# Soft mixture of layer 3: the gate by ScalarE's silu straight into the kept rows, in place of tanh and a product on VectorE

## The chip, the cores and the metric

One core of a Trainium2 chip runs the whole kernel. The metric is the device time of one execution in microseconds. The engines are TensorE (PE in the profile), VectorE (DVE), ScalarE (ACT), GpSimd (POOL) and SyncE (SP), which issues the transfers.

## The reference

Four layers, each `x = x + s * g`, with `s` a mixer over the normalized `x` and `g = silu(f)` with `f` a feed-forward part. `x` is 8 sequences of 512 tokens with 128 features, in float32. In layer 3, `s` is an attention with 16 heads and `f` a soft mixture of 16 experts with 16 slots each:

```python
def _L3_ffn_ref(x, ln_gamma, ln_beta, mu, scale, w1, b1, w2, b2):
    xn = _layernorm(x, ln_gamma, ln_beta)
    x_unit, mu_unit = _l2norm(xn, axis=-1), _l2norm(mu, axis=0)
    logits = jnp.einsum('bnd,des->bnes', x_unit * scale, mu_unit)
    dispatch = jax.nn.softmax(logits, axis=1)
    combine = jax.nn.softmax(logits.reshape(B, N, E * S), axis=-1).reshape(B, N, E, S)
    slot_in = jnp.einsum('bnd,bnes->besd', xn, dispatch)
    h = jax.nn.gelu(jnp.einsum('besd,edh->besh', slot_in, w1) + b1[None, :, None, :], approximate=False)
    slot_out = jnp.einsum('besh,ehd->besd', h, w2) + b2[None, :, None, :]
    return jnp.einsum('besd,bnes->bnd', slot_out, combine)
...
s = _L3_attn_ref(xn, ...)
g = _silu(_L3_ffn_ref(xn, ...))
x = x + s * g
```

## The kernel before

The layers run one after the other. Layer 3 has two stages with a barrier of all engines between them: first the soft mixture (`m3_pe`, `m3_dve`, `m3_act`, `m3_pool`), which leaves the gate of all 8 sequences in `gate3`, then the attention heads (`heads_*`), and at the end `heads_close`, which multiplies the sum over the heads by the gate and adds it to `x`.

The mixture is a pipeline over slots 0 to 13 (`m3_slots`). One sequence `b` goes through it, and in each slot every engine does one step each of several sequences, in an order written out by hand. Waits are semaphore counts: `m3_filled` and `m3_emptied` for the banks of PSUM, and one count for each other kind of result. Buffers are two, taken in turn by `b % 2` (`lanes_m`).

ScalarE's order in slot s is: `open_copy(s-2)` (the transposed rows, L2644), `dispatch_copy(s-2)` (L2674), `combine(s-2)` (four exps with their sums, L2658), `slots_copy(s-2)` (L2680), `units_copy(s-1)` (L2650), `gelu(s-2)` (four, L2686), `dispatch(s-1)` (two exps, L2667), `square(s)` (L2640), `tanh(s-4)` (L2694). A step is left out where its sequence is not one of 0 to 7: so the last `combine` and `gelu` are in slot 9, the last `dispatch` in slot 8, and the gates of sequences 0 to 7 in slots 4 to 11. The program names no tables of ScalarE here; the compiler puts the loads ahead of the functions that need another table.

TensorE's order in a slot is: `slot_logits(s-1)`, `combine_turn(s-2)`, `outputs(s-3)`, `token_logits(s-1)`, `opened_rows(s-1)`, `dispatch_turn(s-1)`, `slots(s-1)`, `slot_out(s-2)`, `units(s)`, `hidden(s-1)`. Of these `slots` waits for ScalarE's `dispatch_copy`, `hidden` for its `slots_copy`, and `slot_logits` for its `units_copy`. Behind the slots stand 16 products of the value and output weights for the heads, in banks 2 to 5, which ScalarE copies out (L2717).

VectorE, in its order, has `dispatch_scale`, `total` (L2542), `token_max`, `moments`, `unit_rows`, `scale`, `gate`, `gamma` (L83), `slot_bias` (L2587), `slot_max` (L2568 and L88), `combine_copy` (L2582) and `divide` (L2596), which writes `f`. GpSimd has `own_expert` (L2782), which stands between gelu and `slot_out`, and small powers.

The gate before is made from tanh: `silu(f) = 0.5 f (1 + tanh(f / 2))`. ScalarE's `tanh(b)` reads `f` (in `sT`) and writes `th` (in `aT`) once `divide(b)` is done and the product of sequence b - 2 has read the buffer. VectorE's `gate(b)` two slots later writes `(th + 1) * f` to `gate3`, twice the gate, and `heads_close` has the factor 0.5.

Of the kernel before, what the change touches and what calls it, by code (L numbers as in the profile page):

```python
# [45 lines left out]
class Kernel:  # L46
# [2186 lines left out]
    def layer3_prepare(self):  # L2233
# [8 lines left out]
        k.own, k.mu_scratch = k.sb("own", [P, 2, P]), k.sb("mu_scratch", [P, 2, 256])  # L2242
        both = k.acc.rearrange("p (two h) t d -> p two (h t) d", two=2)
        k.wv3, k.wo3 = both[:, 0, :, :], both[:, 1, :, :]
        k.m3_mom, k.m3_r, k.m3_norm, k.m3_gt = (n.again() for n in (k.moments, k.rstds, k.scaled, k.gated))
        k.m3_rr, k.m3_xg, k.m3_xb = (Count(nc, n) for n in ("m3_rr", "m3_xg", "m3_xb"))
        k.m3_sq, k.m3_ss, k.m3_ru, k.m3_xu, k.m3_mx, k.m3_ms = (
            Count(nc, n) for n in ("m3_sq", "m3_ss", "m3_ru", "m3_xu", "m3_mx", "m3_ms"))
# [31 lines left out]
        for j in range(2):  # L2280
            half = slice(512 * j, 512 * j + 512)
            quarter = slice(256 * j, 256 * j + 256)
            k.lanes_m.append(dict(
                cmb=flat[:, 1024 * j:1024 * j + 1024].rearrange("p (t c) -> p t c", t=TPB),
                dspT=flat[:, 2048 + 1024 * j:3072 + 1024 * j].rearrange("p (h s) -> p h s", h=2),
                dsp=flat[:, 4096 + 1024 * j:5120 + 1024 * j].rearrange("p (t c) -> p t c", t=TPB),
                cT=flat[:, 6144 + 1024 * j:7168 + 1024 * j].rearrange("p (h s) -> p h s", h=2),
                xn=flat[:, 8192 + 512 * j:8704 + 512 * j].rearrange("p (t d) -> p t d", d=D),
                hT=flat[:, 9216 + 512 * j:9728 + 512 * j],
                g=flat[:, 10240 + 512 * j:10752 + 512 * j].rearrange("p (g s) -> p g s", g=4),  # L2290
                f=k.sT[:, half].rearrange("p (t d) -> p t d", d=D), th=k.aT[:, half].rearrange("p (t d) -> p t d", d=D),
                slotT=k.hT[:, quarter], so=k.hT[:, 512 + 256 * j:768 + 256 * j].rearrange("p (h d) -> p h d", h=2)))
            rows = k.sb(f"m3_rows{j}", [P, 28])
            k.m3_rows.append(dict(r=rows[:, 0:4], r2=rows[:, 4:8], ss=rows[:, 8:12], ru=rows[:, 12:16], mx=rows[:, 16:20],
                                  tot=rows[:, 20:24], ms=rows[:, 24:26], ssum=rows[:, 26:28]))
# [202 lines left out]
    def m3_dve(self):  # L2498
# [97 lines left out]
            V.tensor_tensor(k.lanes_m[j]["f"], k.bank(0).rearrange("p (t d) -> p t d", d=D),  # L2596
                            tot.unsqueeze(2).broadcast_to([P, TPB, D]), ALU.mult).then_inc(*k.m3_emptied[0].up())

        def gate(b):
            t = k.lanes_m[b % 2]  # L2600
            V.wait_ge(k.m3_th.sem, b + 1)
            k.stt(k.gate3[:, b * TPB:(b + 1) * TPB, :], t["th"], 1.0, t["f"], ALU.add, ALU.mult).then_inc(*k.m3_gt.up())

        for s in k.m3_slots():
            if 0 <= s - 3 < SEQS:
                dispatch_scale(s - 3)
            if 0 <= s - 2 < SEQS:
                total(s - 2)
            if 0 <= s - 3 < SEQS:
                token_max(s - 3)  # L2610
            if 0 <= s < SEQS:
                moments(s)
            if 0 <= s - 2 < SEQS:
                unit_rows(s - 2)
            if 0 <= s - 1 < SEQS:
                scale(s - 1)
            if 0 <= s - 6 < SEQS:
                gate(s - 6)
            if 0 <= s - 1 < SEQS:
                gamma(s - 1)  # L2620
            if 0 <= s - 4 < SEQS:
                slot_bias(s - 4)
            if 0 <= s - 2 < SEQS:
                slot_max(s - 2)
            if 0 <= s - 3 < SEQS:
                combine_copy(s - 3)
            if 0 <= s - 4 < SEQS:
                divide(s - 4)

    def m3_act(self):  # L2630
        k, A = self, self.A

        def square(b):
            j = b % 2
            A.wait_ge(k.m3_xb.sem, b + 1)
            k.after(A, k.m3_ss, b - 1)
            if b == 0:
                k.m3_emptied_of(A, 7, "directions")
                A.activation(k.mu_scratch[:, 1, :], k.mu_scratch[:, 1, :], ACT.Sqrt).then_inc(*k.m3_length.up())
            A.activation(k.normed[:, j * TPB:(j + 1) * TPB, :], k.lanes_m[j]["xn"], ACT.Square).then_inc(*k.m3_sq.up())  # L2640

        def open_copy(b):
            k.m3_filled_by(A, 0, "open", b)
            A.activation(k.nT3[:, b, :], k.bank(0), ACT.Identity).then_inc(*k.m3_emptied[0].up())  # L2644

        def units_copy(b):
            k.m3_filled_by(A, 1, "units", b)
            k.m3_filled_by(A, 2, "token_logits", b - 2)
            k.m3_filled_by(A, 4, "slot_logits", b - 2)
            A.activation(k.lanes_m[b % 2]["hT"], k.bank(1), ACT.Identity).then_inc(*k.m3_emptied[1].up())  # L2650

        def combine(b):
            t, r = k.lanes_m[b % 2], k.m3_rows[b % 2]
            A.wait_ge(k.m3_mx.sem, b + 1)
            k.m3_filled_by(A, 2, "combine_turn", b - 2)
            k.m3_emptied_of(A, 0, "outputs", b - 2)
            for i in range(TPB):
                m = A.activation(t["cmb"][:, i, :], k.bank(2 + i // 2)[:, i % 2 * 256:i % 2 * 256 + 256], ACT.Exp,  # L2658
                                 bias=r["mx"][:, i:i + 1], accum_out=r["tot"][:, i:i + 1])
            m.then_inc(*k.m3_emptied[2].up())  # L2660

        def dispatch(b):
            t, r = k.lanes_m[b % 2], k.m3_rows[b % 2]
            A.wait_ge(k.m3_ms.sem, b + 1)
            k.m3_filled_by(A, 4, "dispatch_turn", b - 2)
            for h in range(2):
                m = A.activation(t["dspT"][:, h, :], k.bank(4 + h), ACT.Exp, bias=r["ms"][:, h:h + 1],  # L2667
                                 accum_out=r["ssum"][:, h:h + 1])
            m.then_inc(*k.m3_emptied[4].up())

        def dispatch_copy(b):
            k.m3_filled_by(A, 4, "dispatch_turn", b)
            k.m3_filled_by(A, 1, "slots", b - 2)
            A.activation(k.lanes_m[b % 2]["dsp"].rearrange("p t c -> p (t c)"),  # L2674
                         k.bank(4, 2).rearrange("p a c -> p (a c)"), ACT.Identity).then_inc(*k.m3_emptied[4].up())

        def slots_copy(b):
            k.m3_filled_by(A, 1, "slots", b)
            k.m3_filled_by(A, 6, "hidden", b - 2)
            A.activation(k.lanes_m[b % 2]["slotT"], k.bank(1)[:, 0:256], ACT.Identity).then_inc(*k.m3_emptied[1].up())  # L2680

        def gelu(b):
            k.m3_filled_by(A, 6, "hidden", b)
            k.m3_filled_by(A, 7, "slot_out", b - 2)
            for g in range(4):
                m = A.activation(k.lanes_m[b % 2]["g"][:, g, :], k.bank(6)[:, g * P:(g + 1) * P], ACT.Gelu,  # L2686
                                 bias=k.b1s[:, g:g + 1])
            m.then_inc(*k.m3_emptied[6].up())

        def tanh(b):  # L2690
            t = k.lanes_m[b % 2]
            k.m3_emptied_of(A, 0, "outputs", b)
            k.after(A, k.m3_gt, b - 1)
            A.activation(t["th"], t["f"], ACT.Tanh, scale=0.5).then_inc(*k.m3_th.up())  # L2694

        for s in k.m3_slots():
            if 0 <= s - 2 < SEQS:
                open_copy(s - 2)
            if 0 <= s - 2 < SEQS:
                dispatch_copy(s - 2)  # L2700
            if 0 <= s - 2 < SEQS:
                combine(s - 2)
            if 0 <= s - 2 < SEQS:
                slots_copy(s - 2)
            if 0 <= s - 1 < SEQS:
                units_copy(s - 1)
            if 0 <= s - 2 < SEQS:
                gelu(s - 2)
            if 0 <= s - 1 < SEQS:
                dispatch(s - 1)  # L2710
            if 0 <= s < SEQS:
                square(s)
            if 0 <= s - 4 < SEQS:
                tanh(s - 4)
        for bank in (2, 4):
            k.m3_filled_by(A, bank, "products", bank)
            A.activation(k.wvo[:, 4 * bank - 8:4 * bank, :], k.bank(bank, 2).rearrange("p a (t c) -> p (a t) c", c=D),  # L2717
                         ACT.Identity).then_inc(*k.m3_emptied[bank].up())
# [418 lines left out]
    def heads_close(self):  # L3137
        k, V = self, self.V
        for b in range(SEQS):
            x, s = k.xs[:, b * TPB:(b + 1) * TPB, :], k.acc[:, b, :, :]  # L3140
            V.wait_ge(k.h_acc.sem, k.UNITS - SEQS + b + 1)
            k.step(k.stt(s, s, 0.5, k.gate3[:, b * TPB:(b + 1) * TPB, :], ALU.mult, ALU.mult))
            V.tensor_tensor(x, x, s, ALU.add).then_inc(*k.dve.up())  # L3143
            k.Y.wait_ge(k.dve.sem, k.dve.n)
            k.Y.dma_start(k.io["out"][b].rearrange("(t p) d -> p t d", p=P), x).then_inc(*k.stored.up(16))
# [136 lines left out]
```

## Time and profile before

| | before |
|---|---|
| three executions | 3347.18, 3357.71, 3360.47 us; median 3357.71 |
| the profiled execution | 3347.59 us, span 3345.5 us |
| TensorE, VectorE, ScalarE, GpSimd busy | 93%, 76%, 51%, 25% of the span |
| mixture of layer 3 (1645 to 1775 us of the span) | TensorE 104.9, VectorE 94.0, ScalarE 88.1, GpSimd 54.9 us busy |
| granted clock of TensorE, mean | 0.964 |

The span reaches from the first to the last instruction; the profiled execution took 2.1 us more than its span. Times in the rows are from the start of the span. An engine is busy while it computes, not while it waits for a semaphore.

### The profile page before, as it was taken

What the parts mean: (1) busy time and instruction counts of PE and PEld (TensorE: products, weight loads), DVE (VectorE), ACT (ScalarE), POOL (GpSimd) and SP (SyncE); (2) the same over time, 40 slices, a digit from 0 to 9 for tenths busy, and PEclk for the clock granted to TensorE, in tenths of its full rate; (3) what the DMA queues carried; (4) which work ended last, traced back from release to release, by engine and by line L of the source; (5) the groups of instructions that cost most, each with busy time, mean ns of one, the idle gap of its engine ahead of it and who ended that gap; (6) DMA issues with size and microseconds to landing.
All of it is one profiled execution on the core that took longest, in us unless ns stands there. A gap on an engine that the chain in (4) does not pass through costs nothing. (4 is left out here: it accounts for less than half of the span.)

```text
span 3345.5 us, 57578 instructions
## 1 busy us (share of the span) xinstructions
PE 3112.3 (93%) x20342; PEld 2428.7 (73%) x20342; DVE 2532.5 (76%) x5359; ACT 1702.1 (51%) x3928; POOL 851.6 (25%) x706
## 2 busy tenths in 40 slices
PE   5999998979788789999789999999999999999998
PEld 4777674545454567778577888888888888888887
DVE  4878775858677755555586888888888888888888
ACT  2545543222212144443375666666666666666666
POOL 2101000010101020000243344444444444444443
PEclk9999998989898999998899999999999999999999
DMA  2001101000000000000300010000010110000000
GB/s 53 2 5 51 45 7 48 0 1 1 1 1 0 1 1 1 1 1 1 78 1 1 22 22 22 14 17 15 20 22 22 22 22 9 17 18 22 22 1 26
DMA packets 43552, 53.05 MB, mean 16 GB/s; under 512 B 8645, under 2 KB 27272, under 8 KB 43272
## 3 DMA queue, kind: packets, MB, share of 16 engines
q1 hardware_dynamic: 39298, 47.02, 5.6%
q8 instruction: 167, 2.74, 0.4%
q10 hardware_dynamic: 3974, 2.37, 0.3%
q14 instruction: 113, 0.93, 0.1%
HBM read 38.63 MB, written 10.75 MB: 15 GB/s over the span
## 5 line engine op out<-in xcount | busy, mean ns | idle before, releaser
L75 PE MATMUL banks<-scratch 128*128 128x128 f32 (+3 forms) x3648 | 717.2, 325 | 11.5 <-ACT scratch L2674 8.9
L75 PE MATMUL banks<-nT,w 128*128 128x512 f32 x1184 | 585.5, 613 | 52.7 <-DVE hidden L1562 35.4
L75 PEld LDWEIGHTS banks<-scratch 128*128 128x128 f32 x3648 | 483.9, 192 | 77.4 <-issue 59.7
L75 PEld LDWEIGHTS banks<-scratch,tb 128*128 128x128 f32 x2560 | 356.6, 191 | 101.9 <-issue 61.5
L75 PE MATMUL banks<-scratch,tb 128*128 128x128 f32 x2560 | 368.6, 275 | 0.0
L3117 POOL TENSOR_TENSOR scratch<-scratch,aT 128x1024 f32<-128x1024 f32 x128 | 358.7, 2803 | 4.5 <-DVE aT L2939 4.5
L75 PEld LDWEIGHTS banks<-nT,w 128*128 128x128 f32 x1184 | 204.7, 196 | 212.9 <-issue 145.4
L83 DVE SCALAR_TENSOR_TENSOR scratch<-scratch,tb 128x512 f32<-128x512 f32 (+3 forms) x512 | 339.8, 705 | 8.3
L83 DVE SCALAR_TENSOR_TENSOR scratch<-tb,nn,banks 128x512 f32<-128x512 f32 (+3 forms) x512 | 267.6, 543 | 76.3 <-PE banks L75 72.2
L3109 POOL TENSOR_TENSOR scratch<-backwards,nn 128x512 f32<-128x512 f32 x128 | 133.0, 1039 | 735.7 <-ACT nn L3029 735.7
L2939 DVE TENSOR_TENSOR aT<-banks,turn 64x1024 f32<-64x1024 f32 x256 | 312.9, 1222 | 5.7
L3052 ACT ACTIVATE scratch<-banks 128x384 f32<-128x384 f32 (+1 forms) x384 | 199.7, 520 | 183.5 <-PE banks L79 183.5
L3043 ACT ACTIVATE scratch<-scratch,mn 128x512 f32<-128x512 f32 (+3 forms) x512 | 282.6, 566 | 0.4 <-DVE mn L2973 0.2
L2929 DVE TENSOR_TENSOR scratch<-banks,turn 128x512 f32<-128x512 f32 x256 | 176.1, 688 | 137.7 <-PE banks L75 136.5
L1527 ACT ACTIVATE gated_h<-banks 128x512 f32<-128x512 f32 x160 | 95.5, 597 | 332.2 <-PE banks L75 238.4
L2973 DVE CUSTOM_DVE_ANT_0 scratch<-scratch,tb,coef 128x512 f32<-128x512 f32 (+3 forms) x512 | 261.3, 547 | 0.0
L75 PEld LDWEIGHTS banks<-minus_half,sT 128*128 128x128 f32 x2048 | 239.0, 192 | 2.0 <-ACT sT L3022 2.0
L75 PE MATMUL banks<-minus_half,sT 128*128 128x1 f32 x2048 | 236.1, 245 | 1.2 <-ACT sT L3018 1.2
L79 PEld LDWEIGHTS banks<-ident,scratch 128*128 128x128 f32 x1408 | 171.0, 141 | 73.4 <-issue 69.6
L79 PE MATMUL banks<-ident,scratch 128*128 128x128 f32 x1408 | 219.2, 273 | 3.3 <-DVE scratch L88 2.0
L3035 ACT ACTIVATE scratch<-scratch 128x384 f32<-128x384 f32 (+1 forms) x384 | 215.0, 560 | 8.1 <-DVE scratch L83 6.4
L88 POOL TENSOR_SCALAR rstd<-mv 128x4 f32<-128x4 f32 x40 | 9.9, 247 | 815.6 <-DVE mv L1018 391.1
(393 smaller groups left out, 5367.3 us busy)
## 6 DMA issues: line engine op xcount, KB each, us to landing
tb<-head_rows SPq DMA_DIRECT2D x32, 512.0 KB, 7.1
turn<-head_turns SPq DMA_DIRECT2D x64, 128.0 KB, 2.7
head_turns<-loads SPq DMA_DIRECT2D x16, 256.0 KB, 2.9
head_turns<-rotation SPq DMA_DIRECT2D x16, 256.0 KB, 2.9
xs<-in_x SPq DMA_DIRECT2D x8, 256.0 KB
w<-in_L_Wqk SPq DMA_DIRECT2D x16, 128.0 KB, 2.1
out<-xs SPq DMA_DIRECT2D x8, 256.0 KB, 2.3
w<-in_L_w1T SPq DMA_DIRECT2D x1, 1280.0 KB, 9.2
```

The costliest lines, as they stand in the source:

```text
L75: return self.T.matmul(out, lhsT, rhs, start=start, stop=stop, skip_group_check=True)
L79: return self.T.matmul(out, in_, self.ident[0:n, 0:n], start=start, stop=True, is_transpose=True, skip_group_check=True)
L83: return self.V.scalar_tensor_tensor(out, a, s, b, op0, op1)
L1527: A.activation(k.gated_h[:, u % 2, :], k.bank(2 * (u % 3)), ACT.Tanh, scale=0.5).then_inc(*k.l1_tanh.up())
L2929: V.tensor_tensor(t["qk"][:, i * S:(i + 1) * S], k.bank(2 + i), hd["turn"][:, 0, :], ALU.mult).then_inc(*(k.h_ck if i else k.h_cq).up())
L2939: x = V.tensor_tensor(k.sines[there, :].rearrange("p (i s) -> p i s", i=2), k.bank(2, 2)[here, :, :], hd["turn"][here, 1, :].unsqueeze(1). ...
L2973: x = V.tensor_tensor_reduce(y, y, view(hd["tb"][:, 2, i * P + 127:i * P + 128], [[-1, n]]), k.coef[:, h:h + 1], 3e38, ALU.add, ALU.min, t ...
L3035: A.activation(y, y, ACT.Ln, bias=1.0).then_inc(*k.h_ln.up())
L3043: x = A.activation(y, y, ACT.Exp, bias=t["mn"][:, i:i + 1], scale=-1.0, accum_out=t["sum"][:, i:i + 1])
L3052: A.activation(t["pt"][:, lo:hi], k.bank(7 if piece == 1 else 6)[:, 0:hi - lo], ACT.Identity).then_inc(*k.h_pt.up())
L3109: G.tensor_tensor(t["dk"][:, :, :], k.backwards[:, :].unsqueeze(1).broadcast_to([P, 4, P]), t["nn"][:, 4:8].unsqueeze(2).broadcast_to([P, ...
L3117: G.tensor_tensor(t["qk"], t["qk"], k.sines, ALU.add).then_inc(*k.h_rot.up())
```

## The change

`gate(b)` on VectorE goes. ScalarE's `tanh(b)` becomes `gate(b)`: one silu of `f`, written straight into the rows of `gate3`, which nothing reads before `heads_close`. It waits for `divide(b)` as before and no longer for VectorE's product of sequence b - 2. The buffer `th` and the count `m3_gt` go, and `heads_close` has the factor 1.0. `divide` still waits until ScalarE has read `f` of sequence b - 2.

```diff
-        def gate(b):
-            t = k.lanes_m[b % 2]
-            V.wait_ge(k.m3_th.sem, b + 1)
-            k.stt(k.gate3[:, b * TPB:(b + 1) * TPB, :], t["th"], 1.0, t["f"], ALU.add, ALU.mult).then_inc(*k.m3_gt.up())
...
-            if 0 <= s - 6 < SEQS:
-                gate(s - 6)
...
-        def tanh(b):
+        def gate(b):
             t = k.lanes_m[b % 2]
             k.m3_emptied_of(A, 0, "outputs", b)
-            k.after(A, k.m3_gt, b - 1)
-            A.activation(t["th"], t["f"], ACT.Tanh, scale=0.5).then_inc(*k.m3_th.up())
+            A.activation(k.gate3[:, b * TPB:(b + 1) * TPB, :], t["f"], ACT.Silu).then_inc(*k.m3_th.up())
...
             if 0 <= s - 4 < SEQS:
-                tanh(s - 4)
+                gate(s - 4)
...
-            k.step(k.stt(s, s, 0.5, k.gate3[:, b * TPB:(b + 1) * TPB, :], ALU.mult, ALU.mult))
+            k.step(k.stt(s, s, 1.0, k.gate3[:, b * TPB:(b + 1) * TPB, :], ALU.mult, ALU.mult))
```

## Rows read from the trace of the kernel before

**Rows 1.** The page, busy us and share of the span.

```profile
PE 3112.3 (93%) x20342; PEld 2428.7 (73%) x20342; DVE 2532.5 (76%) x5359; ACT 1702.1 (51%) x3928; POOL 851.6 (25%) x706
```

**Rows 2.** Busy time by stretch: PE, PEld, DVE, ACT, POOL, clock, DMA share, GB/s.

```profile
1645.00:1775.00 130.00, 104.86 (x643) 86.59 (x644) 93.97 (x242) 88.05 (x195) 54.94 (x91) 0.94 0.16 42
```

**Rows 3.** Timeline of ScalarE, one slot: start us, us, line, names, [idle before, releaser].

```profile
1717.74 1.02 ACT L2674 ACTIVATE scratch<-banks 128x1024 f32<-128x1024 f32 x1 [0.28 <-PE banks L79]
1718.66 0.47 ACT L2658 ACTIVATE scratch<-banks,m_rows 128x256 f32<-128x256 f32 x1
...
1720.36 0.22 ACT L2658 ACTIVATION_READ_ACCUMULATOR scratch<-banks,m_rows 128x1 f32 x1
1720.85 0.38 ACT L2680 ACTIVATE hT<-banks 128x256 f32<-128x256 f32 x1 [0.26 <-PE banks L75]
1722.18 0.60 ACT L2650 ACTIVATE scratch<-banks 128x512 f32<-128x512 f32 x1 [0.94 <-PE banks L79]
1722.79 1.28 ACT L2686 ACT_TABLE_LOAD   x1
1724.09 1.14 ACT L2686 ACTIVATE scratch<-banks,b1s 128x128 f32<-128x128 f32 x4
...
1727.88 0.62 ACT L2640 ACTIVATE normed<-scratch 128x512 f32<-128x512 f32 x1
1728.40 0.62 ACT L2694 ACTIVATE aT<-sT 128x512 f32<-128x512 f32 x1
1729.99 0.60 ACT L2644 ACTIVATE nT<-banks 128x512 f32<-128x512 f32 x1 [0.97 <-PE banks L79]
1730.87 1.02 ACT L2674 ACTIVATE scratch<-banks 128x1024 f32<-128x1024 f32 x1 [0.28 <-PE banks L79]
```

**Rows 4.** Timeline of TensorE in that slot: `slots`, `units`, `hidden`, `slot_logits`.

```profile
1718.82 1.99 PE L75 MATMUL banks<-scratch 128*128 128x256 f32 x8 [1.11 <-ACT scratch L2674]
...
1721.54 0.60 PE L79 MATMUL banks<-ident,moe 128*128 128x128 f32 x4
1721.98 1.06 PE L75 MATMUL banks<-hT,w1s 128*128 128x128 f32 x8
1722.87 1.94 PE L75 MATMUL banks<-scratch,mu 128*128 128x512 f32 x4
```

**Rows 5.** Timeline of VectorE in that slot: the product, `slot_max`.

```profile
1721.82 0.68 DVE L83 SCALAR_TENSOR_TENSOR gate<-aT,sT 128x512 f32<-128x512 f32 x1
...
1724.85 1.22 DVE L2568 TENSOR_REDUCE m_rows<-banks 128x2 f32<-128x1024 f32 x1 [0.74 <-PE banks L75]
1726.11 0.17 DVE L88 TENSOR_SCALAR m_rows<-m_rows 128x2 f32<-128x2 f32 x1
```

**Rows 6.** Groups by line, 1645 to 1775 us, and by tile: busy us, mean ns.

```profile
L2667 ACT ACT_TABLE_LOAD x8 | 10.3, 1283 | 0.1
L2686 ACT ACT_TABLE_LOAD x8 | 10.3, 1283 | 0.1
...
L2694 ACT ACTIVATE aT<-sT 128x512 f32<-128x512 f32 x8 | 5.0, 628 | 5.0 <-DVE sT L2596 5.0
...
L83 DVE SCALAR_TENSOR_TENSOR gate<-aT,sT x8: 676/680/691, 1708.7 to 1770.3; 128x512 f32<-128x512 f32 x8
```

**Rows 7.** Timelines of the tail: ScalarE, TensorE (`hidden(7)`, `slot_out(7)`), VectorE.

```profile
1760.62 0.38 ACT L2680 ACTIVATE hT<-banks 128x256 f32<-128x256 f32 x1 [0.26 <-PE banks L75]
...
1762.41 1.14 ACT L2686 ACTIVATE scratch<-banks,b1s 128x128 f32<-128x128 f32 x4
...
1761.31 1.06 PE L75 MATMUL banks<-hT,w1s 128*128 128x128 f32 x8
...
1765.04 1.16 PE L75 MATMUL banks<-w2s,scratch 128*128 128x128 f32 x8
...
1765.73 0.68 DVE L83 SCALAR_TENSOR_TENSOR gate<-aT,sT 128x512 f32<-128x512 f32 x1
1766.33 0.42 DVE L2587 TENSOR_TENSOR hT<-banks,b2s 128x256 f32<-128x256 f32 x1
```

**Rows 8.** The page, DMA issues: KB each, us to landing.

```profile
tb<-head_rows SPq DMA_DIRECT2D x32, 512.0 KB, 7.1
```

More of the change, by code:

```diff
@@ L2244, in layer3_prepare @@
         k.wv3, k.wo3 = both[:, 0, :, :], both[:, 1, :, :]
-        k.m3_mom, k.m3_r, k.m3_norm, k.m3_gt = (n.again() for n in (k.moments, k.rstds, k.scaled, k.gated))
+        k.m3_mom, k.m3_r, k.m3_norm = (n.again() for n in (k.moments, k.rstds, k.scaled))
         k.m3_rr, k.m3_xg, k.m3_xb = (Count(nc, n) for n in ("m3_rr", "m3_xg", "m3_xb"))
@@ L2290, in layer3_prepare @@
                 g=flat[:, 10240 + 512 * j:10752 + 512 * j].rearrange("p (g s) -> p g s", g=4),
-                f=k.sT[:, half].rearrange("p (t d) -> p t d", d=D), th=k.aT[:, half].rearrange("p (t d) -> p t d", d=D),
+                f=k.sT[:, half].rearrange("p (t d) -> p t d", d=D),
                 slotT=k.hT[:, quarter], so=k.hT[:, 512 + 256 * j:768 + 256 * j].rearrange("p (h d) -> p h d", h=2)))
```

## The prediction

> **What bounds the kernel now.** I read the page first. TensorE is busy 93% of the span [rows 1], so a change elsewhere counts only where TensorE waits for it. The table of stretches gives the soft mixture of layer 3 about 130 us out of 3345.5 us, with VectorE at 94.0 and ScalarE at 88.1 us busy in it [rows 2]. Nothing else of the program is touched, apart from a constant (0.5 to 1.0) in `heads_close`, which costs the same. So the question is what sets the length of a slot of this stage.
>
> The timeline of one middle slot answers it. I call its start D: the moment where ScalarE begins `dispatch_copy`, 1717.74, and again 1730.87 in the next slot: a period of 13.13 us [rows 3]. TensorE has one wait in a slot, 1.11 us, for `dispatch_copy` [rows 4]; the rest of the period is its own work end to end, from `slots` over `units`, `hidden`, `slot_logits` to the next `dispatch_turn`. Whatever delays one of these by some time lengthens the slot by that time. ScalarE waits four times in a slot, before `open_copy` 0.97, `dispatch_copy` 0.28, `slots_copy` 0.26 and `units_copy` 0.94 us. One activation starts about 0.10 us ahead of the end of the one before (1717.74 + 1.02 against 1718.66) [rows 3], so the room at each wait is 0.10 us more.
>
> **The work that goes.** Eight `gate` products on VectorE, 0.68 us each [rows 6], at most 5.4 us. In the slot shown the product at 1721.82 stands ahead of `gamma`; behind both VectorE still waits 0.74 us for TensorE's `slot_logits` [rows 5], and TensorE waits for neither. I take nothing for seven of them. If one of VectorE's results set the slot, each would give up to 0.6 us: that is the lower bound. In the tail one counts: the product at 1765.73 holds back `slot_bias(7)` until 1766.33, though `slot_out(7)` is done at 1765.04 + 1.16 = 1766.20 [rows 7]. With 0.04 us for the signal it could start at 1766.24: a gain of 0.09 us. The activation itself stays: eight tanh of 628 ns [rows 6] become eight silu on the same 128x512. I price silu as tanh; an identity of this shape has 0.60 us and the squaring 0.62 us [rows 3], so the function hardly shows in the duration. ScalarE's wait for the product of sequence b - 2 goes too; it never showed as a wait. The stored gate goes straight into rows that nobody reads before the end, so no new wait arises.
>
> **What it adds.** Table loads. Exp and gelu alternate in this stage, and each change has a load of 1283 ns, eight and eight [rows 6]. Tanh has no load of its own at any of its eight places [rows 6], five with exp's table loaded, as in the slot shown [rows 3], and three with gelu's behind the last gelu: both tables have it. Silu does not run in this kernel, so the rows don't show where it lives. Between "as tanh" (no load) and "as gelu" (a load to it and one back), I take the second: a function with a curve of its own, as gelu is.
>
> The order on ScalarE is: combine (exp), gelu, dispatch (exp), squaring, gate. With silu, there is a load ahead of the gate in slots 4 to 9 (in slots 10 and 11 silu is loaded already), and one ahead of combine in slots 5 to 9: 11 loads more. One switch costs the load and the lost overlap: gelu starts 1724.09 - 1722.18 = 1.91 us after `units_copy` rather than 0.50, so 1.41 us [rows 3]. All of it on the path would be 11 x 1.41 = 15.5 us, the upper bound at this price.
>
> The row shows one load of 1.28 us between the copy and gelu, and 0.03 us beside it. The Trainium skill, ScalarE: Activation LUTs, What ACT_TABLE_LOAD costs, has some 2.66 us for a switch, half of it a drain of the engine. The trace agrees with its 1283 ns and shows no such drain. By its price the sum would be +13 us, by the row's the +2.1 us below.
>
> **Step by step in a middle slot, from D.** Combine's first exp moves from D + 0.92 to D + 2.33. The last accumulator read of combine began at 1720.36 = D + 2.62, and the next work can start 0.09 us later, D + 2.71; with the load D + 4.12, where `slots_copy` started at D + 3.11. It ends at D + 4.50, and 0.06 us later (the signal, as 1718.76 to 1718.82) TensorE can start `hidden`: D + 4.56, against 1721.98 = D + 4.24 [rows 3, 4]. So 0.32 us late. `units_copy` could start at D + 4.12 + 0.28 = D + 4.40, before its units are there (D + 4.44): no delay. `slot_logits` goes 0.32 us later with TensorE, then `slot_max` on VectorE, which ended at 1726.11 + 0.17 = D + 8.54 [rows 5]; now D + 8.86, so dispatch starts at D + 8.90 rather than D + 8.80 and pushes the squaring and gate by 0.10 us. The silu load adds 1.41 us: `open_copy` could start at 1728.40 + 0.10 + 1.41 + 0.52 = 1730.43, `dispatch_copy` 0.50 us later, 1730.93 = D + 13.19. TensorE, late by 0.32 us, lets it start only at D + 13.45 [rows 3]. So the silu load is hidden, by 0.26 us, and the load for exp costs 0.32 us a slot.
>
> Slots 5 to 8 have both: 4 x 0.32 = 1.28 us. Slot 4 has the silu load alone: `dispatch_copy` could start at 1730.83 where it started at 1730.87, in the terms of the slot shown: hidden by 0.04 us.
>
> In slot 9 the chain is another [rows 7]: `slots_copy(7)`, gelu(7), `own_expert(7)`, `slot_out(7)`, `slot_bias(7)`, `outputs(7)`, the products of the values. `slots_copy(7)` starts 1.01 us later than 1760.62, ends at 1762.01; the gelu load behind it lets gelu start at 1763.32, against 1762.41 [rows 7]: 0.91 us. Less the 0.09 us at `slot_bias`: 0.82 us. Sum: 1.28 + 0.82 = +2.1 us. VectorE's last products lie beside TensorE's products of the values and end before them, so nothing is gained at the barrier.
>
> The profiled execution has a span of 3345.5 us and took 3347.6 us; it becomes 3349.7 us. That execution stands at the low end of what was run (3347.2 to 3360.5 us), 10.1 us below the median of 3357.7 us. On the median the forecast is 3359.8 us. A measurement of this kernel can't tell under about 0.5% (16.8 us) from no change.
>
> **The rivals.**
>
> *No switch at all.* Silu is in the table that exp uses. Only the 0.09 us at `slot_bias` goes, and perhaps two tenths in slots where VectorE is last: 3357.4 us; with all eight products on the path 5.4 us, 3352.3 us. For it: tanh does just this. Against it: gelu does not, and goes back and forth at every change. Chance 0.12.
>
> *ScalarE becomes the bound.* Its four waits with 0.10 us each leave 2.45 + 0.40 = 2.85 us of room, and two switches take 2.82 us [rows 3]. The period would be 13.13 - 2.85 + 2P for a price P of a switch, beyond the 13.45 us that TensorE sets from P = 1.6 us. If the engine also stood still for as long as a load lasts, P = 2 x 1.283 = 2.57 us, the period would be 15.4 us: 4 x 2.3, with 1.1 us more in slot 4 (2.57 less the 1.45 us of cover there) and 2.0 us in the tail (0.82 and the 1.16 us by which P is dearer) 12.3 us, 3370.0 us. Against it: all 16 loads of the stage last 1283 ns and what follows starts at once. Also here: a load placed ahead of the squaring, which would hold VectorE's `total`; the loads shown stand directly ahead of the function that needs them. Chance 0.08. The Trainium skill's price for a switch (same page and section, an estimate from its 2.66 us) would give 3371 us by the same way.
>
> *Slower by over 0.5%: the load of silu's table is a dear one.* If only the six loads of silu cost Q, the slot is 13.13 - 2.85 + 1.41 + Q = 11.69 + Q, and the whole 4 x (11.69 + Q - 13.13) + (Q - 1.45) + 0.82 = 5Q - 6.4 us. It decides (16.8 us) from Q = 4.6 us. The price could come from a fetch from memory, as a 512 KB transfer with 7.1 us [rows 8]: Q = 1.3 + 7.1 = 8.4 us, +36 us, 3393 us. Against it: the loads of two tables in these rows last 1283 ns alike [rows 6]. The Trainium skill, same page and section, has such a refill by DMA where a program uses more than 8 sets. No run here shows one, and the kernel calls only exp, logarithm, sine, gelu, square root and tanh beside silu. Chance 0.03.
>
> *Faster by over 0.5%.* The stage would need to lose 16.8 us; the removed work is 5.4 us. Only a drift between the measurements does this. Chance 0.02.
>
> **How the numbers follow.** Forecast 0.75, no switch 0.12, ScalarE as bound 0.08, dear load 0.03, faster 0.02. The first three lie within 0.5% and hold 0.95; 0.01 of it goes to slower for drift between measurements: same 0.94, slower 0.04, faster 0.02. The range: the executions of before scatter over 13 us around the same work, so the low end is a low execution with no cost, 3346, and the high end the highest one with half of the bound of 15.5 us, 3360.5 + 7.7 = 3368.
>
> **What would show it.** In the changed profile: six loads at the gate's line and five at combine's, with 8 + 8 as before; a middle slot of 13.45 us (13.13 for no switch, over 15 for a dear switch); the wait of `hidden` for `slots_copy`, about 0.3 us, in three or four slots; `dispatch_copy` still waiting for TensorE; ScalarE's busy time in the stage up by 14 us; VectorE's down by 5.4 us; the heads starting 2.1 us later in the span. I am wrong if the loads stand elsewhere than directly ahead of their function, if silu's activation is longer than 0.63 us by more than 0.26 us, or if there are no new loads.

## The result and the profile after

The changed kernel has a median of 3359.66 us (3354.74 to 3364.81, 22 runs); the kernel before, run between them, 3353.57 us (3347.18 to 3367.18, 22 runs). The ratio is 1.0018, with a 95% interval of 1.0011 to 1.0025: 3.7 to 8.4 us slower, in the band that was called "same", and inside the range. The forecast of 3359.8 us for the median hits by luck: it was 3357.7 us, the median of the three runs known then, plus 2.1 us. The median of before is 3353.6 us over 22 runs, and the change costs more than 2.1 us.

Page of the changed kernel: its span and the first part, to be held against [rows 1].

```profile
span 3358.1 us, 57575 instructions
PE 3123.1 (93%) x20342; PEld 2432.5 (72%) x20342; DVE 2527.6 (75%) x5351; ACT 1717.2 (51%) x3939; POOL 851.1 (25%) x706
```

The profiled span is 12.6 us longer, and most of this is not the change. In the profiled executions TensorE's first matmul of the mixture (`directions`) starts at 1640.6 us before and at 1649.9 us after, behind the same instructions; over all twelve experiments it lies between 1641 and 1655 us, in no order that has to do with the edits. The heads, from their first matmul to the end, take 1571.7 us in both. So I compare the stage alone.

Groups by line of ScalarE, 1645 to 1780 us, changed kernel; the gate is L2686, combine L2651, gelu L2679, dispatch L2660. The last two rows are the gate by tile.

```profile
L2660 ACT ACT_TABLE_LOAD x8 | 10.3, 1283 | 0.1
L2679 ACT ACT_TABLE_LOAD x8 | 10.3, 1283 | 0.1
...
L2686 ACT ACT_TABLE_LOAD x6 | 7.7, 1283 | 0.1
L2651 ACT ACT_TABLE_LOAD x5 | 6.4, 1283 | 0.1
...
L2686 ACT ACTIVATE gate<-sT x8: 629/631/632, 1711.6 to 1782.2; 128x512 f32<-128x512 f32 x8
L83 DVE SCALAR_TENSOR_TENSOR acc<-acc,gate x8: 660/684/685, 3344.1 to 3354.3; 128x512 f32<-128x512 f32 x8
```

Against [rows 6]: six loads at the gate and five at combine, 11 as forecast, each 1283 ns; silu 631 ns, tanh had 628; the product on VectorE is gone. What each part costs was read rightly. What it delays was not.

Timeline of ScalarE in one slot of the changed kernel, which answers to [rows 3]: `dispatch_copy` (L2667), combine with its load, `slots_copy` (L2673), `units_copy` (L2643), gelu, dispatch, the squaring, the gate, `open_copy` (L2637).

```profile
1726.69 1.02 ACT L2667 ACTIVATE scratch<-banks 128x1024 f32<-128x1024 f32 x1
1727.73 1.28 ACT L2651 ACT_TABLE_LOAD   x1
1729.02 0.47 ACT L2651 ACTIVATE scratch<-banks,m_rows 128x256 f32<-128x256 f32 x1
...
1730.84 0.39 ACT L2673 ACTIVATE hT<-banks 128x256 f32<-128x256 f32 x1
1732.04 0.60 ACT L2643 ACTIVATE scratch<-banks 128x512 f32<-128x512 f32 x1 [0.81 <-PE banks L79]
...
1738.38 1.28 ACT L2686 ACT_TABLE_LOAD   x1
1739.68 0.63 ACT L2686 ACTIVATE gate<-sT 128x512 f32<-128x512 f32 x1
1740.21 0.58 ACT L2637 ACTIVATE nT<-banks 128x512 f32<-128x512 f32 x1
1740.73 1.02 ACT L2667 ACTIVATE scratch<-banks 128x1024 f32<-128x1024 f32 x1
```

Timeline of TensorE in the same slot: `slots`, `slot_out`, `units`, `hidden`, `slot_logits`, to be held against [rows 4]. Below it, the row of the chain's wait from the list of who waited for whom (total us, times, longest), 1712.6 to 1769.2 us.

```profile
1727.76 1.99 PE L75 MATMUL banks<-scratch 128*128 128x256 f32 x8 [1.11 <-ACT scratch L2667]
1729.60 1.05 PE L75 MATMUL banks<-w2s,scratch 128*128 128x128 f32 x8
1731.37 0.63 PE L79 MATMUL banks<-ident,moe 128*128 128x128 f32 x4 [0.72 <-ACT hT L2673]
1731.84 1.06 PE L75 MATMUL banks<-hT,w1s 128*128 128x128 f32 x8
1732.73 1.94 PE L75 MATMUL banks<-scratch,mu 128*128 128x512 f32 x4
...
PE banks L79 <- ACT hT L2673: 2.9, 4, 0.7
```

From one `dispatch_copy` to the next it is now 14.04 us, against 13.13. `slots_copy` is at D + 4.15 (D + 4.12 was forecast). But it is `units`, and not `hidden`, that waits for it, 0.72 us in each of four slots: `units` starts at D + 4.68, where it was D + 3.80 (1721.54 in [rows 4]). `slots` and `units` both write bank 1, so `units(s)` has to wait until `slots_copy` has emptied what `slots` left there. `units`, `hidden`, `slot_logits` and all behind them come 0.9 us later.

The list of TensorE's waits ahead of the prediction names `slots`, `hidden` and `slot_logits`, and leaves this one out. In the code it is `take(1)` at the head of `units`, which waits until whatever was written to bank 1 before has been copied out. In the middle slots of the kernel before it was always met in time. In its slot 2, where `slot_out` does not yet stand between `slots` and `units`, the trace of before has it as a row (TensorE, `units`):

```profile
1669.02 0.63 PE L79 MATMUL banks<-ident,moe 128*128 128x128 f32 x4 [0.57 <-ACT hT L2680]
```

The tail of the changed kernel, ScalarE's `slots_copy(7)` and gelu, TensorE's `hidden(7)`, `slot_out(7)`, `outputs(7)` and the products, VectorE's `slot_bias(7)`; D is 1769.21 here and was 1757.52:

```profile
1773.36 0.40 ACT L2673 ACTIVATE hT<-banks 128x256 f32<-128x256 f32 x1
...
1775.07 1.14 ACT L2679 ACTIVATE scratch<-banks,b1s 128x128 f32<-128x128 f32 x4
...
1773.81 1.16 PE L75 MATMUL banks<-hT,w1s 128*128 128x128 f32 x8 [0.63 <-ACT hT L2673]
...
1777.70 1.16 PE L75 MATMUL banks<-w2s,scratch 128*128 128x128 f32 x8
1779.38 2.05 PE L75 MATMUL banks<-hT,scratch 128*128 128x128 f32 x16 [0.52 <-DVE hT L2587]
1781.27 3.74 PE L75 MATMUL banks<-acc 128*128 128x128 f32 x32
...
1778.90 0.42 DVE L2587 TENSOR_TENSOR hT<-banks,b2s 128x256 f32<-128x256 f32 x1 [0.48 <-PE banks L75]
```

Against [rows 7], each from its D: gelu(7) at 5.86 instead of 4.89 (0.97 later, 0.91 was forecast), `slot_bias(7)` at 9.69 instead of 8.81, 0.88 later. The 0.09 us between the two is the wait for the product in [rows 7], which is gone. Little of it is owed to the product's removal: experiment 2 below keeps the product, and there the tail is 0.91 us longer, against 0.89 us here. Once gelu(7) is that late, the product is nearly done when `slot_bias(7)` can start. There is no `units` in the tail, and so it went nearly as forecast. In sum, from `dispatch_copy` in the first full slot (slot 3) to the first product of the values: 94.87 us (1686.40 to 1781.27) against 90.32 us (1678.37 to 1768.69). That is +4.55 us, of which 4 x 0.91 us are the slots and 0.89 us the tail. The stretch starts in slot 3 because slot 2 is disturbed by the clock: before, the eight matmuls of `slots` took 3.65 us there at a mean granted clock of 0.55, in the changed kernel 1.99 us at 1.00, and the slot lasted 14.65 and 12.98 us.

### The profile page after: what moved, and what is told of

The parts are those of the page before. It is cut to its first block and busy times, and to the rows that moved or that the text cites. A ratio compares the mean times of both kernels' runs of the same rounds, so it can differ in the third digit from the quotient of the medians.

```text
span 3358.1 us, 57575 instructions
## 1 busy us (share of the span) xinstructions
PE 3123.1 (93%) x20342; PEld 2432.5 (72%) x20342; DVE 2527.6 (75%) x5351; ACT 1717.2 (51%) x3939; POOL 851.1 (25%) x706
```

## The experiments

Theory A: the eleven loads alone make the stage longer, and only those ahead of combine, because they delay `slots_copy` and bank 1 is shared. Rival B: ScalarE is full, so that the sum of its work counts. Rival C: the product or the write into the kept rows matters. The columns: a middle slot; the stretch from `dispatch_copy` in slot 3 to the first product; and the whole kernel as a ratio to the one before, where timed.

| kernel | slot, us | slot 3 to products, us | whole (95%) |
|---|---|---|---|
| before | 13.13 | 90.32 | |
| changed | 14.04 | 94.87 | 1.0018 (1.0011 to 1.0025) |
| 1: changed, tanh into the rows | 13.13 | 90.24 | |
| 2: before, load at combine | 14.04 | 94.92 | |
| 3: before, load at the gate | 13.13 | 90.33 | |
| 4: changed, `slots` in bank 4 | 13.53 | 92.61 | |
| 5: before, two loads at the gate | 14.37 | 98.53 | |
| 6: before, `slots` in bank 4 | 13.19 | 90.77 | |
| 7: silu at the end | 13.13 | 90.24 | 0.9997 (0.9988 to 1.0006) |
| 8: 7, copy in halves | 13.04 | 89.2 | 0.9988 (0.9980 to 0.9997) |
| 9: 8, own expert first | 12.70 | 87.7 | 0.9982 (0.9971 to 0.9993) |
| 10: 2 again, timed | 14.04 | 94.9 | 1.0003 (0.9994 to 1.0012) |
| 11: changed again | 14.04 | 94.9 | 1.0010 (0.9998 to 1.0021) |
| 12: 2 once more | 14.04 | 94.9 | 1.0008 (0.9995 to 1.0020) |

In 8 and 9 the stretch is taken from `slots` on TensorE (88.55 and 87.06 us, where before has 89.24) plus the 0.65 us from the first half of the copy to it. In 10 to 12 it is taken from `slots` too (93.8 us each) plus 1.08 us.

**1. Tanh straight into the kept rows.** The change without its loads.

```diff
-            A.activation(k.gate3[:, b * TPB:(b + 1) * TPB, :], t["f"], ACT.Silu).then_inc(*k.m3_th.up())
+            A.activation(k.gate3[:, b * TPB:(b + 1) * TPB, :], t["f"], ACT.Tanh, scale=0.5).then_inc(*k.m3_th.up())
```

> The changed kernel with tanh(f/2) in place of silu, written straight into the kept rows: the stored gate is tanh(f/2) and so the output is another. There is neither a product on VectorE nor a new table load. Theory A (the loads alone made the change slower, by way of bank 1: units waits until slots_copy has emptied the bank that slots and units share): a middle slot, from one dispatch_copy to the next, is 13.1 us again as in the kernel before (14.0 in the changed one), and from the first full slot to the products of the values 90.3 us as before (94.9 changed). Rival B (ScalarE is simply full: what counts is the sum of its work) says the same here, 13.1 us. Rival C (the write into the kept rows, or the missing product, costs or gives something): anything other than 13.1 us; with VectorE last somewhere up to 0.6 us a slot less.

13.13 us a slot. The stretch is 0.08 us shorter than before, in the tail, where the prediction had 0.09. The seven other products that VectorE no longer makes give nothing, and the write into the rows costs nothing: rival C is out.

**2. The load at combine alone.**

```diff
+            if 5 <= s <= 9:
+                k.nc.scalar.preload_act_table_set("exp_and_others")
             if 0 <= s - 2 < SEQS:
                 combine(s - 2)
```

> The kernel before, with one more load of exp's table ahead of combine in slots 5 to 9 and nothing else: 5 loads. Theory A: slots_copy starts 1.04 us later, units waits for it, and the slot goes from 13.13 to 14.04 us as in the changed kernel, though the second load is missing; the stage is some 4 x 0.91 plus 0.9 us longer. Rival B: ScalarE has room for one load (2.85 us of waits against 1.41), so the slot stays at 13.1, at most 13.45 us (what the prediction had for hidden).

14.04 us: five of the eleven loads make all of the change. Timeline of ScalarE in a middle slot (combine's load L2702, `slots_copy` L2680, `units_copy` L2650, `open_copy` L2644), and the wait on bank 1 (1710.7 to 1752.9 us: total, times, longest):

```profile
1724.81 1.02 ACT L2674 ACTIVATE scratch<-banks 128x1024 f32<-128x1024 f32 x1 [0.28 <-PE banks L79]
1725.85 1.28 ACT L2702 ACT_TABLE_LOAD   x1
...
1728.96 0.39 ACT L2680 ACTIVATE hT<-banks 128x256 f32<-128x256 f32 x1
1730.16 0.60 ACT L2650 ACTIVATE scratch<-banks 128x512 f32<-128x512 f32 x1 [0.81 <-PE banks L79]
...
1737.98 0.60 ACT L2644 ACTIVATE nT<-banks 128x512 f32<-128x512 f32 x1 [0.97 <-PE banks L79]
1738.86 1.02 ACT L2674 ACTIVATE scratch<-banks 128x1024 f32<-128x1024 f32 x1 [0.28 <-PE banks L79]
...
PE banks L79 <- ACT hT L2680: 2.2, 3, 0.7
```

ScalarE still waits 0.81, 0.97 and 0.28 us in this slot, so it is not full, and the slot is as long as in the changed kernel. Rival B does not hold.

**3. The load at the gate alone.**

```diff
+            if 4 <= s <= 9:
+                k.nc.scalar.preload_act_table_set("exp_and_others")
             if 0 <= s - 4 < SEQS:
                 tanh(s - 4)
```

> The kernel before, with one more load of exp's table ahead of tanh in slots 4 to 9 and nothing else: 6 loads. Theory A: the load fits into the room ahead of open_copy and dispatch_copy (1.45 us), the slot stays at 13.13 us and the stage grows by under 0.3 us. Rival B: one load of two costs half of the 0.91 us, 13.6 us a slot; and if A and B are both wrong and this load is the one that costs, 14.0 us.

13.13 us and 90.33 us: six loads for nothing. Timeline of ScalarE, from the load to the next `dispatch_copy`:

```profile
1742.47 1.28 ACT L2714 ACT_TABLE_LOAD   x1
1743.77 0.63 ACT L2694 ACTIVATE aT<-sT 128x512 f32<-128x512 f32 x1
1744.30 0.58 ACT L2644 ACTIVATE nT<-banks 128x512 f32<-128x512 f32 x1
1744.82 1.02 ACT L2674 ACTIVATE scratch<-banks 128x1024 f32<-128x1024 f32 x1
```

The waits of 0.97 and 0.28 us are gone from it; the load fills them, and `dispatch_copy` is no later for it, as the prediction had it.

**4. `slots` in bank 4**, which `dispatch_copy` has just emptied; all waits that name the bank of `slots` follow.

```diff
         def slots(b):
...
-            to = take(1)
+            to = take(4)
...
-            filled(m, 1, "slots", b)
+            filled(m, 4, "slots", b)
```

> The changed kernel, with slots written to bank 4 (which dispatch_copy has just emptied) in place of bank 1, which it shared with units. All 11 loads stay. Theory A: units no longer waits for slots_copy, units_copy starts at D + 4.4 again, and only hidden, which reads what slots_copy wrote, is late by 0.32 to 0.36 us: a slot of 13.45 to 13.5 us, the number that the prediction gave. Rival B: the work on ScalarE is the same, so the slot stays at 14.0 us.

13.53 us with all eleven loads in place. Timeline of TensorE: `slots`, `slot_out`, `units`, `hidden`:

```profile
1730.64 1.97 PE L75 MATMUL banks<-scratch 128*128 128x256 f32 x8 [1.21 <-ACT scratch L2667]
1732.44 1.05 PE L75 MATMUL banks<-w2s,scratch 128*128 128x128 f32 x8
1733.33 0.60 PE L79 MATMUL banks<-ident,moe 128*128 128x128 f32 x4
1734.06 1.16 PE L75 MATMUL banks<-hT,w1s 128*128 128x128 f32 x8
```

`units` no longer waits, and `hidden` starts 0.73 us behind it instead of 0.44: the 0.3 us of the prediction. The kernel that the prediction described is this one, and not the one that was timed. Not all of its sum holds even here: the loads lengthen slots 5 to 7, but slot 8 lasts 13.59 us here and 13.59 us in experiment 6, which has the same bank and no loads. The stretch is 1.84 us longer than in experiment 6 (92.61 against 90.77), where the prediction had 2.1 us.

**5. Two loads at the gate**, gelu's table and then exp's, as the check on the room there.

```diff
+            if 4 <= s <= 9:
+                k.nc.scalar.preload_act_table_set("gelu_and_others")
+                k.nc.scalar.preload_act_table_set("exp_and_others")
```

> The kernel before, with two loads (gelu's table, then exp's) ahead of tanh in slots 4 to 9. One load there was free. Theory A: the room ahead of open_copy and dispatch_copy is 1.45 us, two loads take 1.41 + 1.30 = 2.7 us, so ScalarE now holds dispatch_copy and a slot is 13.13 + 1.25 = 14.4 us. Rival (loads at this place cost nothing at all, whatever their number, because something else is always later): 13.13 us.

14.37 us, 1.24 us more than before; 1.25 was forecast from a room of 1.45 us. So the third experiment came out free because of the room, and not because a load at this place is free.

```profile
1731.87 1.28 ACT L2714 ACT_TABLE_LOAD   x1
1733.16 1.28 ACT L2715 ACT_TABLE_LOAD   x1
1734.46 0.63 ACT L2694 ACTIVATE aT<-sT 128x512 f32<-128x512 f32 x1
1734.99 0.58 ACT L2644 ACTIVATE nT<-banks 128x512 f32<-128x512 f32 x1
```

**6. The kernel before with `slots` in bank 4**, by the same edit as in 4.

> The kernel before, with slots in bank 4 as in the fourth experiment, no load added: what the move itself costs. Theory A with the 0.06 us that slots 2 and 3 of the fourth experiment showed: 13.19 us in all slots, since dispatch_copy and slots_copy are now one after the other on one bank and the wait of slots is 0.09 us longer. If the move costs nothing by itself: 13.13 us.

13.19 us: the move itself costs 0.06 us. Taken off the 13.53 us of the fourth experiment it leaves 13.47, against the 13.45 us of the prediction.

**7. Silu at the end.** Keeps the change's idea and takes the loads out of the slots.

```diff
-            k.after(V, k.m3_th, b - 1)
-            V.tensor_tensor(k.lanes_m[j]["f"], ...
+            V.tensor_tensor(k.gate3[:, b * TPB:(b + 1) * TPB, :], ...
...
-        def gate(b):
+        def gate(lo, hi):
+            g = k.gate3[:, lo * TPB:hi * TPB, :]
+            k.m3_emptied_of(A, 0, "outputs", hi - 1)
+            A.activation(g, g, ACT.Silu)
...
-            if 0 <= s - 4 < SEQS:
-                gate(s - 4)
+            if s >= 9 and s - 3 <= SEQS:
+                gate(0 if s == 9 else s - 4, s - 3)
```

> The changed kernel, with silu out of the slots: divide writes f straight into the kept rows, and ScalarE applies silu there in place, to the first six sequences at once in slot 9 behind the last gelu and to the last two in slots 10 and 11. One load more than before in place of 11, no product on VectorE, and 0.5 us less on ScalarE in each of the slots 4 to 8. Theory A: slots of 13.13 us as before, from the first full slot to the products 90.2 us (before 90.3, changed 94.9), and the whole the same as before within what can be measured (ratio 0.999 to 1.001). A rival by which the freed work of VectorE and ScalarE counts: up to 0.6 us a slot less, 87 to 88 us. Another, by which the silu of six sequences (2.7 us) holds the end: 92 us.

13.13 us, 90.24 us, ratio 0.9997. Timeline of ScalarE at the end: the load, and six sequences and the seventh in one row, ahead of the wait for the last `divide`.

```profile
1765.08 1.28 ACT L2685 ACT_TABLE_LOAD   x1
1766.37 3.28 ACT L2685 ACTIVATE gate<-gate 128x3072 f32<-128x3072 f32 x2
1771.11 0.63 ACT L2685 ACTIVATE gate<-gate 128x512 f32<-128x512 f32 x1 [1.45 <-DVE gate L2595]
```

The freed work of VectorE and ScalarE (a product and an activation a slot) is worth nothing here.

**8. The same, with `dispatch_copy` in halves**, aimed at the one wait that TensorE has in a slot.

```diff
+            A.activation(to[:, 0:512], k.bank(4), ACT.Identity).then_inc(*k.m3_half.up())
+            A.activation(to[:, 512:1024], k.bank(5), ACT.Identity).then_inc(*k.m3_emptied[4].up())
...
-            k.m3_emptied_of(T, 4, "dispatch_turn", b)
+            T.wait_ge(k.m3_half.sem, b + 1)
...
             for t in range(TPB):
+                if t == 2:
+                    k.m3_emptied_of(T, 4, "dispatch_turn", b)
```

> The seventh experiment, with dispatch_copy in two halves, bank 4 and then bank 5, and slots starting on the first. TensorE's only wait in a slot, 1.11 us for dispatch_copy, should become about 0.7 us: ScalarE's first half lasts 0.6 us in place of 1.02. If this wait is the whole slack of the loop, as theory A has it: a slot of 12.7 us, the stage 3.3 us shorter than before, ratio 0.999. If ScalarE's or VectorE's loop is as long as TensorE's: 13.1 us still.

A miss in size: 13.04 us and not 12.7, for the wait fell to 0.69 us but `slot_out` then started late. TensorE's `slots` and `slot_out`, the weight load of `slot_out`, and GpSimd's `own_expert` (L2776):

```profile
1709.20 1.99 PE L75 MATMUL banks<-scratch 128*128 128x256 f32 x8 [0.69 <-ACT scratch L2669]
1711.27 1.16 PE L75 MATMUL banks<-w2s,scratch 128*128 128x128 f32 x8
...
1711.27 0.97 PEld L75 LDWEIGHTS banks<-w2s,scratch 128*128 128x128 f32 x8 [0.48 <-POOL scratch L2776]
...
1709.92 1.30 POOL L2776 TENSOR_TENSOR scratch<-scratch,own 128x512 f32<-128x512 f32 x1 [0.35 <-POOL m_rows L88]
```

`own_expert` ends at 1711.22, and `slot_out` starts at 1711.27: the row of its weight load names the wait, the matmul's own row does not. In the kernel before, `own_expert` ended at 1720.40, 0.25 us ahead of `slot_out` (1720.65): again a wait that had been met in time, right behind the one that was shortened.

**9. `own_expert` ahead of `unit_power`** in GpSimd's order, in the kernel of 8.

```diff
-            if 0 <= s - 1 < SEQS:
-                unit_power(s - 1)
             if 0 <= s - 3 < SEQS:
                 own_expert(s - 3)
+            if 0 <= s - 1 < SEQS:
+                unit_power(s - 1)
```

> The eighth experiment gave 13.04 us a slot and not 12.7: the wait for dispatch_copy fell from 1.11 to 0.69 us, but slot_out then waited for own_expert on GpSimd, which stands behind unit_power there. Here own_expert(s - 3) goes ahead of unit_power(s - 1) in GpSimd's order; its gelu is done 8 us earlier. Theory A: slot_out follows slots without a gap, the slot is 12.7 us, from the first full slot to the products 87.5 us (before 90.3), ratio to before 0.999. Rival: the next wait (VectorE's unit_rows, or slots_copy on bank 1) stands right behind, and the slot stays above 12.9 us.

12.70 us as forecast, in slots 3 to 6; slot 7 has 13.10 us, with a wait of 0.49 us for VectorE's `combine_copy`. The stretch is 87.7 us (87.5 was forecast), the whole 0.9982 (0.9971 to 0.9993): 2.3 to 9.7 us faster than the kernel before. The gain comes from TensorE's wait and not from silu, for experiment 7, with silu alone, had none. The stage is 2.6 us shorter than before; the middle of the interval, 6 us, is more than that, and I do not claim it.

**10, 11 and 12. The whole kernel once more.** The load at combine, timed; then it and the changed kernel beside each other.

> The second experiment once more, now timed: the kernel before and five loads ahead of combine. The changed kernel measured a ratio of 1.0018 (1.0011 to 1.0025), 3.7 to 8.4 us, where its stage in the trace is 4.6 us longer. Theory A: these five loads are all of it, and the whole kernel is slower by the same 4.6 us, ratio 1.0014. If the change costs something outside the stage too (about 1.5 us, if the middle of its interval is taken at its word), this kernel comes out below the changed one, at 1.0010 or less.

> The changed kernel once more, beside the kernel before and the five loads of the next run on one chip. The stage is 4.6 us longer in the trace, the whole measured 1.0018 (1.0011 to 1.0025). The stretch ahead of the mixture, with the same instructions in every kernel here, ended between 1640.6 and 1654.5 us in the profiled executions, so a whole-kernel ratio can be off by some microseconds. Theory A: 1.0014, within 1.0005 to 1.0023, and the stage 4.6 us longer again. If the changed kernel costs something more outside the stage, it comes out at 1.0018 or above again.

> The kernel before with five loads ahead of combine, a third time. Timed before it gave 1.0003 (0.9994 to 1.0012), below the 1.0014 that its own stage (4.6 us longer) asks for. Theory A, with the scatter ahead of the mixture as the reason: the stage 4.6 us longer again, and the whole near 1.0014, alike with the changed kernel of the same call. If there is something outside the stage that tells the two kernels apart: 1.0003 again here, and 1.0018 there.

The tenth run missed: the stage is 4.6 us longer, which would be 1.0014, and the whole measured 1.0003, with an interval (0.9994 to 1.0012) that leaves 1.0014 out. In 11 and 12 the same kernel gave 1.0008 and the changed one 1.0010, with both intervals holding 1.0014 and no difference between the two. So nothing outside the stage tells them apart that these runs could show. The scatter ahead of the mixture, 14 us over the profiled executions, is three times as large as what is asked for.

The granted clock accounts for most of that scatter. Two stretches ahead of the mixture, first in the kernel before and then in the changed one (after the five engines' busy times: granted clock, DMA share, GB/s):

```profile
1200.00:1400.00 200.00, 195.81 (x1384) 153.03 (x1383) 110.07 (x211) 87.23 (x144) 8.25 (x12) 0.94 0.00 1
1200.00:1400.00 200.00, 195.83 (x1328) 151.26 (x1327) 106.72 (x207) 85.70 (x141) 8.25 (x12) 0.91 0.00 1
```

TensorE is as busy in both, but at 0.91 it got through fewer matmuls (1328 against 1384). Added up from the clock records of the traces, TensorE stood at the lower of its two levels (1.2 GHz) for 215 us ahead of the mixture in the kernel before, 232 us in the changed one and 245 us in experiment 3, and the mixture began at 1640.6, 1649.9 and 1654.5 us. Over the 14 traces each further microsecond at the lower level goes with 0.47 us of time, to within 1 us in most of them and 2.4 us in the worst. What makes one execution stand there longer than another stays open.

## Why the prediction was right in its range and wrong in its sum

- **What bounds a slot** (TensorE's own work and its wait for `dispatch_copy`): right. Experiments 8 and 9 shortened the wait and the slot followed, once `slot_out` was freed too.
- **The removed work** (nothing but 0.09 us in the tail): right, 0.08 us in experiment 1. Beside the loads even this is hardly gained: 0.89 us of tail in the changed kernel, 0.91 us in experiment 2, which keeps the product.
- **Silu needs loads, 11 of 1283 ns, at 1.41 us each:** right in number, place and length. The ground given, that silu is a curve of its own as gelu is, was an analogy, and tanh in the same rows spoke against it; that it came out was in part luck.
- **The load at the gate is hidden:** right; experiments 3 and 5 show the room to be 1.45 us. The margin was another: 0.26 us was forecast, since TensorE alone was to be late. `units_copy` is late by the same 0.91 us, so the room stays 1.45 us against a load of 1.41 us, and 0.04 us are left.
- **The load at combine costs 0.32 us a slot:** this term was wrong. It is 0.91 us. The failed step is "`units_copy` could start at D + 4.12 + 0.28 = D + 4.40, before its units are there (D + 4.44): no delay". It took the time of `units` as fixed. `units` waits for `slots_copy` too, since the two share bank 1. In the kernel before it starts 0.31 us behind the end of `slots_copy` (1721.54 against 1720.85 + 0.38), a wait that was met by then and so left no row in the slot that was read. It did leave one in slot 2 of the same trace, 0.57 us, shown above. With `slots` in bank 4 the 0.32 us came true (0.34 us a slot, 13.53 against 13.19), in three slots of four.
- **The tail** (0.82 us): right to 0.07 us, 0.89 us; gelu(7) was 0.97 us late and not 0.91.
- **The sum:** 4 x 0.91 + 0.89 = 4.5 us instead of 2.1 us; whole kernel 3.7 to 8.4 us, and -0.7 to 7.0 us in the repetition.
- **The rivals:** there was a switch; its price was 1.41 us, so neither the dear load nor ScalarE as the bound came in. In the changed kernel ScalarE does come close: it waits only 0.81 us in a slot, and its own chain from `units_copy` to `dispatch_copy`, 8.69 us, is as long as TensorE's. But experiment 2 has the same slot with two more waits in it.
- **What was to be seen:** "the wait of `hidden` for `slots_copy`, about 0.3 us, in three or four slots" was wrong by name and size; `hidden` has such a wait only in the tail, 0.63 us. The middle slot of 13.45 us did not come, and neither did "`dispatch_copy` still waiting for TensorE": at 1726.69 and 1740.73 it starts right behind `open_copy`. What came are the eleven loads where they were forecast, silu as long as tanh, ScalarE's busy time from `directions` to the heads up by 14.15 us (88.80 to 102.95) and VectorE's down, by 4.9 us (95.44 to 90.53) where 5.4 was forecast. The heads started 12.6 us later and not 2.1, most of it from ahead of the mixture.

## What to carry to other kernels

Count the table loads that a function brings from the order of the functions, not from its own line: the expensive load here stood at combine, which the change did not touch. When an eviction is delayed, ask who writes that bank next, beside who reads the result; a wait that is met 0.3 us early leaves no row in that slot, so read the first slots of a pipeline too, where fewer steps stand between the two. And judge a change of a few microseconds by the stage that it is in, with a kernel that adds only the suspected cost; the whole kernel scatters by more.

## What the runs showed of the hardware

- A load of a table that is active already takes the same 1283 ns and delays as much: the load at combine in experiment 2 (exp's table, active) gave the slot of the changed kernel to 0.01 us. Of two loads in a row (experiment 5), the second starts 1.29 us after the first, and the activation 1.30 us after the second.
- The silu activation on 128x512 takes 631 ns, tanh 628 ns. Six sequences in one activation (128x3072) and a seventh behind it take 3.28 us together.
- Silu's table is neither the one active behind exp nor the one active behind gelu: it has its load in slots 4 to 8, behind dispatch's exp, and in slot 9, behind the last gelu (six loads at the gate). Exp has a load behind silu in turn (five, at combine). Tanh has none behind either.
- The same instructions took 1640.6 to 1654.5 us up to the mixture in 14 profiled executions, with 215 and 245 us of it at the lower level of the granted clock at the two ends.
